# A mixed attention and state-space layer: six of sixteen u*B products on GpSimd, softmax divided after P*V, small norm steps on VectorE, x loaded batch by batch

## Chip, cores and metric
One core of one Trainium2 chip. The time is the device time of one execution in microseconds (us), the median of several runs. The profiled execution is a single one; its span is given beside its time.

## What is computed
Eight independent sequences (batches) of 512 tokens with D = 128 channels, float32. Each goes through one layer of four branches and one feed-forward step:

```
xn    = normalise(x); delta = softplus(xn W_dt + b)          # state-space branch, NS = 64 states
h     = scan over t of  exp(-exp(A_log) delta_t) h + (delta_t xn_t) B_t ;  y_t = sum_n h_tn C_tn
attn  = 16 heads of 8, blocks of 32 queries on 96 keys, softmax(scores + bias) V, then W_o
conv  = silu(4-tap causal convolution);  mem = x W_wm + 0.3 softmax(x dec^T) dec
x1    = x + 0.2 attn + 0.45 (y + x D) W_ssm + 0.15 conv + 0.2 mem
out   = x1 + normalise(x1) W2 + bias                         # W2: quantised kernel plus low rank
```

## The kernel before
**Units and slots.** The recurrence has 128 x 64 = 8192 rows, done as 64 units of 128 rows (two channels with 64 states each). In every batch a unit needs: u = delta*xn of its two channels spread over 64 partitions each (on TensorE, `unit_u`, line 903, into one of four PSUM banks `uP`), the product u*B (`unit_input`, 1182, VectorE), the decay exp(A*delta) (`unit_exp`, 657, ScalarE, from rows that the DMAs `widen`, 393, have written 64 times), the scan itself (`unit_scan`, 1191, VectorE), and the product with C (`pair_product`, 1384, GpSimd, for two units at a time), which TensorE sums (`reduce_group`, 930). Units with s % 4 == 3 do not use TensorE and VectorE for u*B: `widen_u` (382) brings their u by DMA into `uwide`, and `pool_input` (1398) multiplies on GpSimd.

**Order by hand.** Each engine's program goes through slots s = 0..63 of a batch (`body`), and everything else of the layer hangs on a slot: the tables `AT`, `JOB_AT`, `SCORES_AT` and the lags behind a block's scores slot (lines 46 to 78). VectorE's slot s is: waits for scores if a block's bias is due (`scores_there`, 1205), `unit_input(s)`, `unit_scan(s-1)`, then small things: `bias_and_max`, `inverse_sums`, memory softmax, norms. TensorE's slot s begins with `unit_u(s+2)`, which waits for the scan of unit s-2, since the bank is used again; ScalarE's with `unit_exp(s+2)`, which waits for scan s-1. All waits are on counting semaphores, in program order: whatever stands behind a waiting instruction on its engine waits too. Batches 1 to 6 are a loop of three turns with two batches each; batches 0 and 7 stand in front of and behind it.

**Attention.** Block k (of 16) has its scores in slot 6+3k on TensorE (bank `sP`), bias and maximum on VectorE in slot +2, exp on ScalarE in +3 and +4, the inverse of the sums on VectorE in +6 (`inverse_sums`, 1219), the division of all 384 probabilities per query on GpSimd from +5 (`prob_norm`, 1392), transposes on TensorE in +9 and their copy on ScalarE, P*V in +11 and its copy (`ao_copy`, 691). At the end of the batch four matmuls with `wo_p` (`project`, n = 6 to 9, line 998) read the result.

**Norms.** `ln_stats` (1155) and `ln_aggr` on VectorE in slots 0 and 2 treat the next batch's x, `ln_root_step` (1367) does eight 128x4 steps on GpSimd in slots 4 to 7, `ln_apply` (541) follows on ScalarE in slot 11. The second norm: `residual` (1241) in slot 14, `aggr2` 16, `root2` (1407, four steps, GpSimd) 17, `normalise2` (548, ScalarE) 20.

**x.** All eight batches of x are loaded at the start (`x_load`, 353, lines 372 and 373) and stay in SBUF. SyncE issues nearly all DMAs, in one program order: its `front` (475) ends with twelve `window_values` DMAs, and then comes `body`.

Of the kernel before, what the change touches and what calls it, by code (L numbers as in the profile page):

```python
# [5 lines left out]
F32 = mybir.dt.float32  # L6
# [44 lines left out]
LAST_PROJECT = {60: (0, 1), 61: (2, 3), 62: (4, 5), 63: (6, 7)}  # L51
# [5 lines left out]
    "normalise2": 20, "ffn": 25, "output": 29,  # L57

    "ln_stats": 0, "ln_aggr": 2, "ln_root": 4, "ln_apply": 11, "scale_xn": 12, "softplus_exp": 20,
# [8 lines left out]
ROWS_AT = {"store": 15, "rows": 14}  # L68
VALUE_DMA_AT = {4: (0, 1, 2, 3, 4, 5), 5: (6, 7, 8), 6: (9, 10, 11)}
# [7 lines left out]
BIAS_LAG, EXP_LAG, INV_LAG, NORM_LAG, PT_LAG, PT_COPY_LAG, PV_LAG, AO_COPY_LAG = 2, (3, 4), 6, 5, 9, 9, 11, 11  # L77
# [8 lines left out]
def memory_tile_at(s, lag):  # L86
# [7 lines left out]
    ["stats", "aggr", "ve", "nm", "r", "nb", "vr", "vrr", "ve2", "r2", "xa", "xn"])}  # L94
# [4 lines left out]
POOL_Q = 3  # L99
UNIT_PAIRS = UNITS // 2  # L100
# [9 lines left out]
L2 = {n: i + 1 for i, n in enumerate(["x1", "stats", "aggr", "ve", "nm", "r", "nb", "z"])}  # L110
# [5 lines left out]
def hybrid_block_kernel(nc, x, ln_g, ln_b, w_xproj, w_dt, b_dt, A_log, D_ssm, w_ssm_out, wq, wk, wv,  # L116
# [3 lines left out]
    with ctx:  # L120
# [14 lines left out]
        mhalf = sb("mhalf", [128, NT])  # L135
        mone = sb("mone", [128, NT])
        eps_t = sb("eps_t", [128, NT])
# [9 lines left out]
        wo_p = sb("wo_p", [128, REP, D])  # L147
# [32 lines left out]
        x_sb = sb("x_sb", [128, NB, NT, D])  # L180
        st = sb("st", [128, NT, 6])
        mv = sb("mv", [128, NT, 2])
        ve = sb("ve", [128, NT])
        rr = sb("rr", [128, NT])
        vr = sb("vr", [128, NT])
        rr2 = sb("rr2", [128, NT])
        nm = sb("nm", [128, NT])
# [18 lines left out]
        u_rows = nc.dram_tensor("u_rows", [2, 32, L], F32, kind="Internal").ap()  # L206
        uwide = [sb(f"uwide{c}", [128, 2, L]) for c in range(U_SLOTS)]
        q_mask = sb("q_mask", [128, REP])
# [10 lines left out]
        prob = sb("prob", [128, 4, KVH, 3 * W])  # L219
# [3 lines left out]
        ao4 = sb("ao4", [128, REP, L])  # L223
# [16 lines left out]
        nmz = sb("nmz", [128, NT])  # L240
# [4 lines left out]
        x_in = [sem(f"x_in{i}") for i in range(2)]  # L245
# [13 lines left out]
        p_exp, p_inv, p_norm = sem("p_exp"), sem("p_inv"), sem("p_norm")  # L259
        pt_ready, pt_evac, pv_ready, ao_evac = sem("pt_ready"), sem("pt_evac"), sem("pv_ready"), sem("ao_evac")  # L260
# [6 lines left out]
        urows_out, gbx_done = sem("urows_out"), sem("gbx_done")  # L267
        uwide_in = [sem(f"uwide_in{c}") for c in range(U_SLOTS)]
        head_tables = sem("head_tables")
# [13 lines left out]
        def job_count(fam, B, name):  # L283
            return B * COUNT[fam] + INDEX[fam][name] + 1

# [32 lines left out]
        N_FIRST_DMA, N_W_DMA = 13, 18  # L318

        def xin(B):  # L320
            if isinstance(B, int):
                return x_sb[:, B, :, :]
            return x_sb[:, bass.ds(B, 1), :, :].rearrange("p a t d -> p (a t) d")
# [28 lines left out]
        def _(sp):  # L352
            def x_load(b):
                sp.dma_start(x_sb[:, b, :, :], x[b].rearrange("(t p) d -> p t d", p=128)) \
                    .then_inc(x_in[min(b, 1)], 16)

            x_load(0)
# [14 lines left out]
            for b in range(1, NB):  # L372
                x_load(b)


            def store_rows(B, p):

                wait(sp, sp_step, B * N_SP + SP["u"])
                sp.dma_start(dt_rows[p], dtv[:, :]).then_inc(rows_out, 16)
                sp.dma_start(u_rows[p], uv[32 * POOL_Q:32 * POOL_Q + 32, :]).then_inc(urows_out, 16)  # L380

            def widen_u(B, p, m):

                wait(sp, scan_done, B * UNITS + 8 * (m - U_SLOTS) + 8)
                if m == 0:
                    wait(sp, urows_out, (B + 1) * 16)
                flat = u_rows.rearrange("a d t -> (a d t)")
                for j in range(2):
                    row = p * 32 + 4 * m + j
                    src = bass.AP(flat.tensor, flat.offset + row * L, [[0, 64], [2 * L, 2], [1, L]])  # L390
                    sp.dma_start(uwide[m % U_SLOTS][64 * j:64 * j + 64, :, :], src).then_inc(uwide_in[m % U_SLOTS], 16)

# [11 lines left out]
            def body(B, p):  # L404
                for m in range(UNIT_PAIRS):
# [19 lines left out]
            def load_weights():  # L425
# [12 lines left out]
                sp.wait_ge(const_ready, 2)  # L438
                for g in range(KVH):
                    sp.dma_start(wo_p[32 * g:32 * g + HD, :, :],  # L440
                                 wo[g * REP * HD:(g + 1) * REP * HD, :].rearrange("(r h) e -> h r e", r=REP)) \
                        .then_inc(w_in, 16)
                    n += 1
                assert n == N_W_DMA

            def window_values(B, which):
# [4 lines left out]
                else:  # L451
                    wait(sp, s_ready, B * NBLK + 1)
# [22 lines left out]
            def front(B, p):  # L475
# [23 lines left out]
        def _(act):  # L499
# [14 lines left out]
            def setup_step(s):  # L514

                if s == 0:
                    act.wait_ge(w_in, 16 * N_W_DMA)
# [23 lines left out]
            def ln_apply(B):  # L541
                wait(act, ln_step, B * N_LN + LN["r2"])
                for t in range(NT):
                    ins = nc.scalar.activation(xa[:, t, :], xin(B)[:, t, :], ACT.Identity, bias=nb[:, t:t + 1],
# [12 lines left out]
            def scale_xn(B):  # L557
                wait(act, ln_step, B * N_LN + LN["xa"])
                for t in range(NT):
                    ins = nc.scalar.activation(xn[:, t, :], xa[:, t, :], ACT.Copy, scale=rr2[:, t:t + 1])  # L560
# [96 lines left out]
            def unit_exp(B, s):  # L657
# [6 lines left out]
                to = uP[q][:, :] if q == POOL_Q else decay[:, q, :]  # L664
# [9 lines left out]
            def probabilities(B, k, half):  # L674
                if half == 0:
                    wait(act, s_max, B * NBLK + k + 1)
                    wait(act, pt_ready, B * NBLK + k - 3)
                for g in (2 * half, 2 * half + 1):
                    ins = nc.scalar.activation(prob[:, k % 4, g, :], s_sb[:, k % 2, g, :], ACT.Exp,  # L679
# [11 lines left out]
            def ao_copy(B, k):  # L691
                wait(act, pv_ready, B * NBLK + k + 1)
                if k == 0:
                    wait(act, ready["t"], B * N_TAIL - N_TAIL + 1)
                nc.scalar.activation(ao4[:, :, k * W:(k + 1) * W],  # L695
                                     ptP[:, 0:128].rearrange("p (r q) -> p r q", r=REP), ACT.Copy).then_inc(ao_evac, 1)
# [55 lines left out]
            def body(B, p):  # L752
                for s in range(UNITS):
# [6 lines left out]
                    else:  # L760
                        if s == AT["y_copy"]:
# [12 lines left out]
                    k = block_at(s, AO_COPY_LAG)  # L774
                    if k is not None:
                        ao_copy(B, k)
# [27 lines left out]
            def tail(B, p):  # L804
                y_copy(B)
# [8 lines left out]
        def _(pe):  # L814
# [8 lines left out]

            pe.wait_ge(const_ready, 1)
# [6 lines left out]
            def setup_step(s):  # L831

                if s == 0:
                    pe.wait_ge(w_in, 16 * N_W_DMA)
# [68 lines left out]
            def unit_u(B, p, s):  # L903

                i, q = divmod(s, 4)
                if q == POOL_Q:
# [33 lines left out]
            def scores(B, p, k):  # L940
                if k == 0:
                    wait(pe, done["p"], job_count("p", B, "k"))
                wait(pe, s_max, B * NBLK + k)
                mm(sP[:, 0:KVH * 3 * W], q4[:, k, :, :].rearrange("p r q -> p (r q)"), k4[:, :, k * W:k * W + 3 * W],  # L944
                   start=True, stop=True).then_inc(s_ready, 1)

            def prob_transposes(B, k):
                wait(pe, p_norm, B * NBLK + k + 1)
                wait(pe, ao_evac, B * NBLK + k)
# [520 lines left out]
```

## Time and profile before

| | us |
|---|---|
| median of 3 runs (1114.25 to 1122.23) | 1114.3 |
| the profiled execution | 1114.23 |
| its span in the profile | 1112.4 |

So 1.8 us lie around the span. Batches 1 to 6 begin on VectorE at 176, 308, 439, 571, 704 and 834 us, and batch 7 at 963: some 131 to 132 us for each batch, or 2.05 us for a slot. In the profile DVE is VectorE, ACT ScalarE, POOL GpSimd, PE TensorE and SP SyncE; an arrow `<-` in brackets names what ended an idle time.

### The profile page before, as it was taken

The page shows a single profiled execution, that of the slowest core. Times are in us where ns is not written, and L with a number is a line of the kernel's source. Part 1 is how long each engine was busy: PE and PEld are TensorE (multiplying, and loading weights), DVE is VectorE, ACT ScalarE, POOL GpSimd, SP SyncE. Part 2 cuts the span into 40 slices and gives each one's busy share as a digit, 9 for nine tenths or more (in the row PEclk, how much of TensorE's full clock was granted, in tenths as well). Part 3 has the DMA queues.
Part 4 walks back from the last instruction along what each step waited for, and adds up shares of the span by engine and source line. Part 5 has one row for each costly group of instructions (what it writes and reads, how often), then busy time and mean ns, then how long its engine had stood idle before and what let it go on. Part 6 is the DMA issues. An engine that isn't in the chain of part 4 may idle for free. (4 is left out here: it accounts for less than half of the span.)

```text
span 1112.4 us, 19145 instructions
## 1 busy us (share of the span) xinstructions
PE 830.9 (75%) x4151; PEld 339.3 (30%) x4151; DVE 979.3 (88%) x2299; ACT 837.5 (75%) x2255; POOL 955.6 (86%) x675
## 2 busy tenths in 40 slices
PE   5367878688777786877778777867868778677775
PEld 2023333233323332333323333323332333232332
DVE  2688999979997999979999699897999799999991
ACT  4468886788778878687877887679887887858871
POOL 6369988989898988988899898899989898979892
PEclk9556998978997989979898798888899798989897
DMA  5845667647675666666676476665666566766630
GB/s 111 196 126 169 180 159 185 171 138 198 163 183 155 185 167 159 172 157 172 168 203 161 128 191 162 167 173 159 177 176 183 153 187 165 188 161 164 196 95 9
DMA packets 124391, 181.18 MB, mean 163 GB/s; under 512 B 29263, under 2 KB 41056, under 8 KB 124256
## 3 DMA queue, kind: packets, MB, share of 16 engines
q1 hardware_dynamic: 123968, 179.56, 61.4%
q14 instruction: 96, 0.79, 0.3%
q8 instruction: 39, 0.64, 0.3%
q10 hardware_dynamic: 288, 0.20, 0.1%
HBM read 170.79 MB, written 5.05 MB: 158 GB/s over the span
## 5 line engine op out<-in xcount | busy, mean ns | idle before, releaser
L1389 POOL TENSOR_TENSOR prod<-hst,C 128x1024 f32<-128x1024 f32 x256 | 602.0, 2354 | 94.9 <-DVE hst L1201 94.4
L1201 DVE TENSOR_TENSOR_SCAN hst<-decay,bank 128x512 f32<-128x512 f32 x384 | 459.5, 1209 | 3.0 <-DVE cv_a L1236 2.8
L1189 DVE TENSOR_TENSOR bank<-bank,B 128x512 f32<-128x512 f32 x384 | 263.1, 685 | 52.6 <-PE bank L911 34.8
L665 ACT ACTIVATE decay<-wide,A_rep 128x512 f32<-128x512 f32 x384 | 273.4, 715 | 41.5 <-DVE hst L1201 31.2
L911 PE MATMUL bank<-spread,sel_bc 96*128 96x512 bf16 x384 | 164.5, 434 | 101.0 <-DVE hst L1201 90.6
L679 ACT ACTIVATE prob<-s_sb,nmax 128x96 f32<-128x96 f32 x512 | 185.2, 365 | 0.9 <-DVE nmax L1214 0.5
L1405 POOL TENSOR_TENSOR uwide<-uwide,B 128x512 f32<-128x512 f32 x128 | 162.7, 1271 | 22.5 <-DMA uwide<-u_rows 22.5
L935 PE MATMUL bank<-prod,sel_red 128*32 128x512 f32 x1024 | 164.9, 722 | 0.0
L1201 DVE TENSOR_TENSOR_SCAN hst<-bank,uwide 128x512 f32<-128x512 f32 x128 | 155.4, 1214 | 2.7 <-POOL uwide L1405 2.7
L951 PE MATMUL bank<-ident,prob 128*96 128x128 f32 x512 | 85.9, 295 | 77.5 <-ACT ao L695 58.3
L944 PE MATMUL bank<-k,q 128*128 128x384 f32 x256 | 126.7, 580 | 22.3 <-DVE nmax L1214 22.2
L688 ACT ACTIVATE probT<-bank 96x512 f32<-96x512 f32 x128 | 74.9, 585 | 72.0 <-PE bank L951 71.6
L911 PEld LDWEIGHTS bank<-spread,sel_bc 96*128 96x128 bf16 x384 | 40.2, 106 | 228.0 <-DVE hst L1201 176.5
L665 ACT ACTIVATE bank<-wide,A_rep 128x512 f32<-128x512 f32 x128 | 87.2, 681 | 26.8 <-DVE hst L1201 26.6
L1394 POOL TENSOR_TENSOR prob<-prob,pinv 128x384 f32<-128x384 f32 x128 | 105.8, 826 | 0.0
L951 PEld LDWEIGHTS bank<-ident,prob 128*96 128x96 f32 x512 | 61.3, 137 | 135.4 <-issue 102.6
L1214 DVE CUSTOM_DVE_ANT_0 s_sb<-bank,bias 128x96 f32<-128x96 f32 x512 | 98.3, 250 | 0.0
L679 ACT ACTIVATION_READ_ACCUMULATOR prob<-s_sb,nmax 128x1 f32 x512 | 98.1, 192 | 0.0
L944 PEld LDWEIGHTS bank<-k,q 128*128 128x128 f32 x256 | 48.9, 216 | 87.0 <-DVE nmax L1214 48.6
L959 PE MATMUL bank<-probT,vw 96*8 96x128 f32 x1024 | 57.0, 298 | 14.7 <-ACT probT L688 9.8
L695 ACT ACTIVATE ao<-bank 128x128 f32<-128x128 f32 x128 | 34.1, 266 | 30.8 <-PE bank L959 30.5
L959 PEld LDWEIGHTS bank<-probT,vw 96*8 96x8 f32 x1024 | 19.9, 94 | 89.5 <-issue 57.1
(189 smaller groups left out, 1027.4 us busy)
## 6 DMA issues: line engine op xcount, KB each, us to landing
wide<-dt_rows SPq DMA_DIRECT2D x512, 256.0 KB, 4.7
uwide<-u_rows SPq DMA_DIRECT2D x128, 256.0 KB, 4.1
spread<-parts SPq DMA_DIRECT2D x66, 32.0 KB, 4.1
x_sb<-in_L_attn_x_dram SPq DMA_DIRECT2D x8, 256.0 KB, 4.5
dt_rows<-sp_t SPq DMA_DIRECT2D x8, 256.0 KB, 2.6
out_dram<-outb SPq DMA_DIRECT2D x8, 256.0 KB, 3.9
vw<-v_tok SPq DMA_DIRECT2D x80, 16.0 KB, 3.3
u_rows<-uv SPq DMA_DIRECT2D x8, 64.0 KB, 2.4
```

The costliest lines, as they stand in the source:

```text
L665: nc.scalar.activation(to, wide[m % SLOTS][:, s % 2, :], ACT.Exp, scale=A_rep[:, g:g + 1]).then_inc(exp_done, 1)
L679: ins = nc.scalar.activation(prob[:, k % 4, g, :], s_sb[:, k % 2, g, :], ACT.Exp, bias=nmax[:, k % 2, g:g + 1], scale=-1.0, accum_out=psum ...
L911: mm(uP[q][:, :], sel_bc[:, i, :, :].rearrange("k j n -> k (j n)"), spread[p][:, q, :], start=True, stop=True).then_inc(u_ready, 1)
L935: ins = mm(yP[32 * q:32 * q + 32, :], sel_red[:, i, :], prod[:, (i % 2) * 4 + q, :], start=(i == 0), stop=(i == GROUPS - 1), skip_group_ch ...
L944: mm(sP[:, 0:KVH * 3 * W], q4[:, k, :, :].rearrange("p r q -> p (r q)"), k4[:, :, k * W:k * W + 3 * W], start=True, stop=True).then_inc(s_ ...
L951: ins = nc.tensor.transpose(ptP[0:3 * W, g * 128:(g + 1) * 128], prob[:, k % 4, g, :], ident[:, :])
L1189: v.tensor_tensor(uP[s % 4][:, :], uP[s % 4][:, :], B2[p][:, :], ALU.mult).then_inc(dbx_done, 1)
L1201: v.tensor_tensor_scan(hst[:, s % 8, :], kept, into[:, :], 0.0, ALU.mult, ALU.add).then_inc(scan_done, 1)
L1214: ins = v.tensor_tensor_reduce(s_sb[:, k % 2, g, :], sP[:, g * 3 * W:(g + 1) * 3 * W], bias3[:, row, g, :], 1.0, BIG, ALU.add, ALU.min, nm ...
L1389: g.tensor_tensor(prod[:, 2 * (m % 4):2 * (m % 4) + 2, :], hst[:, 2 * (m % 4):2 * (m % 4) + 2, :], C2[p][:, :].unsqueeze(1).to_broadcast([ ...
L1394: g.tensor_tensor(prob[:, k % 4, :, :], prob[:, k % 4, :, :], pinv[:, k % 4, :].unsqueeze(2).to_broadcast([128, KVH, 3 * W]), ALU.mult) \
L1405: g.tensor_tensor(u, u, B2[p][:, :], ALU.mult).then_inc(gbx_done, 1)
```

## The change
- GpSimd takes u*B of the units s % 8 == 5 as well (24 of 64, before 16). Their u comes through a second DRAM table and `widen_odd` into `uodd`. In each batch that is eight products more on GpSimd, and eight products fewer on VectorE and eight matmuls fewer on TensorE. In an odd slot GpSimd does `pair_product`, then the product of unit s+4 (in slots s % 8 == 1), then that of s+6 (in slots s % 4 == 1).
- GpSimd's division of the probabilities goes. P*V runs on raw exponentials at lag 8 (transposes at lag 6), `raw_copy` takes it to SBUF, TensorE turns it (`turn`, lag 10) into the unused fourth quarter of the bank `sP`, and VectorE divides 32 values per query (`output_norm`, lag 11). At the end of the batch `heads` transposes back, `heads_copy` copies, and sixteen matmuls of 128 columns replace four of 512.
- Because the turned block lies in the bank of the scores, VectorE's `scores_there` also waits for `turned`, from the fourth block on.
- `inverse_sums` moves from lag 6 to 8.
- The norms' steps, all but the power, go to VectorE: `ln_vars` (slots 4 to 7), `ln_shift` (10), `vars2` (16), `shift2` (20); GpSimd keeps one power for each norm (slots 7 and 17). `ln_stats` moves to slot 1, `ln_apply` to 12, `normalise2` to 21.
- x is kept for one batch: SyncE loads x of the next batch at the start of `body`, and x again into `x1` for the residual in its step 21.
- The output weights go to a larger tile `wo4`, cleared on VectorE and loaded by 16 DMAs at the end of SyncE's `front`.

```diff
+def on_pool(s):
+    return s % 4 == 3 or s % 8 == 5
...
-BIAS_LAG, EXP_LAG, INV_LAG, NORM_LAG, PT_LAG, PT_COPY_LAG, PV_LAG, AO_COPY_LAG = 2, (3, 4), 6, 5, 9, 9, 11, 11
+BIAS_LAG, EXP_LAG, INV_LAG, PT_LAG, PT_COPY_LAG, PV_LAG, RAW_COPY_LAG, TURN_LAG, NORM_LAG = 2, (3, 4), 8, 6, 6, 8, 8, 10, 11
+TURN_AHEAD = 3
...
-            for b in range(1, NB):
-                x_load(b)
...
             def body(B, p):
+                if not last(B):
+                    x_load(B + 1, x_sb, x_in)
                 for m in range(UNIT_PAIRS):
...
+                    if m % 8 == 7:
+                        if m // 8 + 2 < 4:
+                            widen_odd(B, p, m // 8 + 2)
+                        elif not last(B):
+                            widen_odd(B + 1, 1 - p, m // 8 - 2)
...
+                    if m == ROWS_AT["residual"]:
+                        x_load(B, x1, xres_in)
...
                 for m in range(U_SLOTS):
                     widen_u(B, p, m)
+                    widen_odd(B, p, m)
                 for at in VALUE_DMA_AT.values():
                     window_values(B, at)
+                load_output_weights()
...
+            def turn(B, k):
+                wait(pe, raw_evac, B * NBLK + k + 1)
+                wait(pe, ao_norm, B * NBLK + k)
+                nc.tensor.transpose(sP[:, KVH * 3 * W:], ao_raw[:, k % 2, :], ident[:, :]).then_inc(turned, 1)
...
             def ln_stats(B):
-                dve.wait_ge(x_in[0], 16)
-                if not first(B):
-                    dve.wait_ge(x_in[1], 16 * (NB - 1))
+                wait(dve, x_in, B * 16 + 16)
...
                 wait(dve, s_ready, B * NBLK + k + 1)
                 wait(dve, p_exp, B * NBLK + k - 1)
+                if k >= TURN_AHEAD:
+                    wait(dve, turned, B * NBLK + k - TURN_AHEAD + 1)
...
+            def output_norm(B, k):
+                wait(dve, turned, B * NBLK + k + 1)
+                wait(dve, p_inv, B * NBLK + k + 1)
+                wait(dve, heads_ready, B)
+                v.tensor_tensor(ao_q[:, k, :].rearrange("p (g h) -> p g h", h=HD),
+                                sP[:, KVH * 3 * W:].rearrange("p (g c) -> p g c", c=W)[:, :, 0:HD],
+                                pinv[:, k % 4, :].unsqueeze(2).to_broadcast([128, KVH, HD]), ALU.mult).then_inc(ao_norm, 1)
...
+            def shift2(B):
+                wait(dve, l2_step, B * N_L2 + L2["r"])
+                v.scalar_tensor_tensor(nbz[:, :], mv2[:, :, 0], -1.0, rz[:, :], ALU.mult, ALU.mult).then_inc(l2_step, 1)
```

## Rows read from the trace of the kernel before
**Rows 1.** The page, part 1: busy time, share of the span, instructions
```profile
PE 830.9 (75%) x4151; PEld 339.3 (30%) x4151; DVE 979.3 (88%) x2299; ACT 837.5 (75%) x2255; POOL 955.6 (86%) x675
```
**Rows 2.** Waits of VectorE over the whole span: total us, times, longest
```profile
DVE bank L1189 <- PE bank L911: 34.8, 24, 8.1
DVE pinv L1222 <- ACT prob L679: 25.3, 8, 3.8
DVE bank L1189 <- PE bank L944: 14.3, 14, 2.4
```
**Rows 3.** Groups of instructions by line and shape: busy us, mean ns | idle before
```profile
L1189 DVE TENSOR_TENSOR bank<-bank,B 128x512 f32<-128x512 f32 x384 | 263.1, 685 | 52.6 <-PE bank L911 34.8 <-PE bank L944 14.3 <-issue 1.8
L1405 POOL TENSOR_TENSOR uwide<-uwide,B 128x512 f32<-128x512 f32 x128 | 162.7, 1271 | 22.5 <-DMA uwide<-u_rows 22.5
L1394 POOL TENSOR_TENSOR prob<-prob,pinv 128x384 f32<-128x384 f32 x128 | 105.8, 826 | 0.0
L1375 POOL TENSOR_TENSOR rr<-ve,mhalf 128x4 f32<-128x4 f32 x8 | 8.1, 1014 | 0.1
L1222 DVE RECIPROCAL pinv<-psum_r 128x4 f32<-128x4 f32 x128 | 20.0, 156 | 25.3 <-ACT prob L679 25.3
```
**Rows 4.** Timeline of VectorE at the start of batch 4: start, us, instruction
```profile
569.81 1.20 DVE L1201 TENSOR_TENSOR_SCAN hst<-bank,uwide 128x512 f32<-128x512 f32 x1
571.51 0.86 DVE L1160 BATCH_NORM_STATS2 st<-x_sb 128x6 f32 x4
...
579.58 0.70 DVE L1189 TENSOR_TENSOR bank<-bank,B 128x512 f32<-128x512 f32 x1 [0.70 <-PE bank L911]
...
585.47 0.70 DVE L1189 TENSOR_TENSOR bank<-bank,B 128x512 f32<-128x512 f32 x1 [0.69 <-PE bank L911]
```
**Rows 5.** Timeline of SyncE at the same place, and where the loop turns (437 us)
```profile
571.04 1.22 SPq L391 DMA_DIRECT2D uwide<-u_rows  x2
...
437.59 1.23 SPq L391 DMA_DIRECT2D uwide<-u_rows  x2
443.47 6.02 SPq L402 DMA_DIRECT2D wide<-dt_rows  x8
```
**Rows 6.** Line 354, the eight loads of x: from issue to landing
```profile
DMA to landing us min/median/max: 2.9/4.5/6.4
```
**Rows 7.** Timeline of SyncE in the front
```profile
22.04 1.36 SPq L440 DMA_DIRECT2D wo_p<-in_L_attn_wo_dram x4
...
37.38 2.55 SPq L391 DMA_DIRECT2D uwide<-u_rows  x4
40.05 8.43 SPq L456 DMA_DIRECT2D vw<-v_tok  x12
```
**Rows 8.** Timeline of VectorE in batch 0
```profile
40.39 0.17 DVE L1115 MEMSET bias<- 128x128 f32 x1
...
46.96 1.22 DVE L1201 TENSOR_TENSOR_SCAN hst<-bank,uwide 128x512 f32<-128x512 f32 x1 [2.73 <-POOL uwide L1405]
...
51.52 1.45 DVE L1121 TENSOR_SCALAR wo_p<-wo_p 128x512 f32<-128x512 f32 x1
...
63.05 0.29 DVE L1133 TENSOR_REDUCE wmax<-wf_abs 128x1 f32<-128x128 f32 x1 [2.60 <-ACT wf_abs L532]
```
**Rows 9.** Timeline of batch 3: GpSimd's product of slot 17, VectorE's first of slot 21
```profile
475.95 2.36 POOL L1389 TENSOR_TENSOR prod<-hst,C 128x1024 f32<-128x1024 f32 x1 [2.12 <-DVE hst L1201]
...
479.28 0.70 DVE L1189 TENSOR_TENSOR bank<-bank,B 128x512 f32<-128x512 f32 x1
```
**Rows 10.** Timeline of TensorE in slots 39 and 40 of batch 3, then VectorE in slot 41
```profile
524.27 0.60 PE L951 MATMUL bank<-ident,prob 128*96 128x128 f32 x4
524.71 1.88 PE L967 MATMUL bank<-xaT,convdiag 128*128 128x512 f32 x4
526.42 0.38 PE L911 MATMUL bank<-spread,sel_bc 96*128 96x512 bf16 x1
...
525.66 0.68 DVE L1189 TENSOR_TENSOR bank<-bank,B 128x512 f32<-128x512 f32 x1
```

More of the change, by code:

```diff
@@ L99, with products @@
 POOL_Q = 3
+def on_pool(s):
+    return s % 4 == 3 or s % 8 == 5
+def products(s, pool):
+    return sum(on_pool(t) == pool for t in range(s + 1))
+N_POOL = sum(on_pool(s) for s in range(64))
+N_VEC = 64 - N_POOL
 UNIT_PAIRS = UNITS // 2
@@ L146, in hybrid_block_kernel @@
         wk_s = sb("wk_s", [D, KVH * HD])
-        wo_p = sb("wo_p", [128, REP, D])
+        wo4 = sb("wo4", [128, 4, REP, D])
         w_ssm = sb("w_ssm", [D, D])
@@ L436, in load_weights, with load_output_weights @@
                     n += 1
[L438 to L443, printed above, removed]
-                assert n == N_W_DMA
+                assert n == N_W_DMA
+            def load_output_weights():
+                sp.wait_ge(wo_clean, 1)
+                for c in range(4):
+                    for g in range(KVH):
+                        sp.dma_start(wo4[32 * c + g * HD:32 * c + g * HD + HD, c, :, :],
+                                     wo[g * REP * HD:(g + 1) * REP * HD, :].rearrange("(r h) e -> h r e", r=REP)) \
+                            .then_inc(w_in, 16)
             def window_values(B, which):
@@ L689, in probT_copy, with raw_copy, heads_copy @@
                     .then_inc(pt_evac, 1)
-            def ao_copy(B, k):
+            def raw_copy(B, k):
                 wait(act, pv_ready, B * NBLK + k + 1)
[L693 to L696, printed above, removed]
+                wait(act, turned, B * NBLK + k - 1)
+                nc.scalar.activation(ao_raw[:, k % 2, :], ptP[:, 0:128], ACT.Copy).then_inc(raw_evac, 1)
+            def heads_copy(B):
+                wait(act, heads_ready, B + 2)
+                nc.scalar.activation(aoT[:, :, :, :].rearrange("p c r q -> p (c r q)"), ptP[:, :], ACT.Copy,
+                                     scale=RW_ATTN).then_inc(heads_evac, 1)
             def mem_exp(B, t):
@@ L960, in values, with heads @@
                 ins.then_inc(pv_ready, 1)
+            def turn(B, k):
+                wait(pe, raw_evac, B * NBLK + k + 1)
+                wait(pe, ao_norm, B * NBLK + k)
+                nc.tensor.transpose(sP[:, KVH * 3 * W:], ao_raw[:, k % 2, :], ident[:, :]).then_inc(turned, 1)
+            def heads(B):
+                wait(pe, ao_norm, (B + 1) * NBLK)
+                transposes([ao_q[:, 4 * a:4 * a + 4, :].rearrange("p k c -> p (k c)") for a in range(4)], 128, 128, ptP) \
+                    .then_inc(heads_ready, 1)
             def conv_tap(B, p, tap):
@@ L998, in project @@
                 elif n < 10:
-                    wait(pe, ao_evac, (B + 1) * NBLK)
-                    ins = mm(jobP[:, :], wo_p[:, n - 6, :], ao4[:, n - 6, :], start=False, stop=False)
+                    wait(pe, heads_evac, B + 1)
+                    c = n - 6
+                    for r in range(REP):
+                        ins = mm(jobP[:, :].rearrange("p (a c q) -> p a c q", a=4, c=4)[:, :, c, :], wo4[:, c, r, :],
+                                 aoT[:, :, r, :], start=False, stop=False, skip_group_check=True)
                 else:
@@ L1056, in body @@
                         values(B, p, k)
+                    k = block_at(s, TURN_LAG)
+                    if k is not None:
+                        turn(B, k)
+                    if s == UNITS - 1:
+                        heads(B)
                     for tap in range(TAPS):
@@ L1073, in tail @@
             def tail(B, p):
-                for n in range(8, N_PROJ - 1):
+                for n in range(6, N_PROJ - 1):
                     project(B, p, n)
@@ L1176, in front @@
                 ln_aggr(B)
+                for n in range(4):
+                    ln_vars(B, n)
+                ln_shift(B)
                 first_tables()
@@ L1289, in body @@
                         inverse_sums(B, k)
+                    k = block_at(s, NORM_LAG)
+                    if k is not None:
+                        output_norm(B, k)
                     t = memory_tile_at(s, M_MAX_LAG)
@@ L1315, in tail @@
                 aggr2(B)
+                vars2(B)
+                shift2(B)
                 output(B)
@@ L1416, in body @@
                         pair_product(B, p, s // 2)
-                    if s % 4 == 1:
-                        if s // 4 + 1 < GROUPS:
-                            pool_input(B, p, s // 4 + 1)
-                        elif not last(B):
-                            pool_input(B + 1, 1 - p, 0)
-                    k = block_at(s, NORM_LAG)
-                    if k is not None:
-                        prob_norm(B, k)
+                    for ahead in (4, 5, 6):
+                        t = s + ahead
+                        if s % 2 == 1 and (t == s + 6 and t % 4 == 3 or t == s + 4 and t % 8 == 5):
+                            if t < UNITS:
+                                pool_input(B, p, t)
+                            elif not last(B):
+                                pool_input(B + 1, 1 - p, t - UNITS)
                     if not first(B):
```

216 lines of the change are left out of this document (123 added, 93 removed).

## Prediction
> **What bounds the kernel now.** Read the page's part 1 first: VectorE is busy 88% of the span, GpSimd 86%, ScalarE and TensorE 75% [rows 1]. Two engines near 90% leave open which one paces the other, so next come VectorE's waits over the span. The reader is to see that none of the large ones is for GpSimd: 34.8 us for TensorE's spread of u (8.1 of it in the front), 25.3 for the exponentials (one wait in each batch, at the inverse of the sums), 14.3 for the scores [rows 2]. GpSimd on its side waits for scans, once 2.12 us [rows 9]. So VectorE paces the body, disturbed by a late TensorE and ScalarE, and GpSimd follows. A microsecond taken from GpSimd is worth nothing by itself; one taken from VectorE is worth one, as long as TensorE and ScalarE can follow; and each new wait in VectorE's program costs in full.
>
> **Part 1, VectorE's own work.** Eight products fewer in each batch. One lasts 0.685 us [rows 3], but the next instruction starts 0.58 after it, so 8 x 0.59 = 4.7 us go. Sixteen `output_norm` of 128x32 come. No row has one; below is the reciprocal of 128x4, 0.156 long and about 0.07 from start to start, above the product of 512 elements at 0.59. The work is nearest to the small one, 32 elements: I take 0.09, so 1.4; the range for sixteen is 1.1 to 3. The norms bring seven small steps at 0.07 to 0.15, 0.7 with one self-wait. Net -2.5 us per batch, -20 over eight.
>
> **Part 2, GpSimd.** It loses sixteen divisions (0.826), gains eight products (1.271) and loses one of three powers (1.01) and nine smaller steps: -13.2 + 10.2 - 1.0 = -4 us per batch, and a little more for the small steps [rows 3]. As VectorE does not wait for it, I cost this at nothing. The cover: the product of unit s+4 ends 2.3 + 1.2 = 3.5 us after scan s, and scan s+4 starts four slots of 2.05 us less its own 1.2 later, 7 us. The Trainium skill (GPSIMD Engine Reference, "Performance versus the Vector engine") speaks against handing such work over: elementwise work should stay on VectorE, GpSimd takes about twice as long. The trace agrees, 1.271 against 0.685 [rows 3]; but the rule prices the engine, and here the dearer microseconds fall on the engine that nobody waits for.
>
> **Part 3, x arrives late.** Until now x was in SBUF. Now its load stands at the start of SyncE's `body`, behind `widen_u` and `widen_odd` of step 31, and the former waits for the last scan of the batch. In batch 4 that scan ends at 571.0 and SyncE issues at 571.04, two DMAs in 1.22 us [rows 4, 5]. Four DMAs, then x: issued at 573.5. x landed in 2.9 to 6.4 us, median 4.5 [rows 6]; with four 256 KB transfers ahead of it I take 4.0: 577.5. VectorE reaches `ln_stats` in slot 1, after one product and one scan more than before: 571.51 + 0.58 + 1.13 = 573.2. It stands for 4.2 us. At the turn of the loop (two of six) SyncE resumed its next DMA only 4.65 us after the end of the last [rows 5]; if that is the turn itself, x comes that much later, some 7 us of waiting. Batch 1 about 3. Sum over batches 1 to 6: 3 + 3 x 4.2 + 2 x 7 = 29.6. Some comes back: while VectorE stands, TensorE works off its projections, and its three waits behind them (the first 0.70, the last 0.69, one of 0.45 between) go [rows 4]: -10. Net +20; both ends: +6 (landing in 2.9 and no turn penalty) and +32. The Trainium skill's page on DMA (DMA: Bandwidth & Descriptors, "Rules for kernel authors") says to issue early and wait late; the change issues and waits within 3 us. No rule of it changes the sum.
>
> **Part 4, batch 0.** This one is larger than any other and the surest. x of batch 1 is now issued after all of SyncE's front. Before, that was four `uwide` DMAs from 37.38 and twelve `vw` in 8.43 us. Now it is eight of the former (4 x 0.61 more), then sixteen of `wo4` at 0.34, 5.4 us [rows 7]: 37.4 + 4.9 + 8.4 + 5.4 = 56.1, landing at about 60. VectorE is ready for it when its bias tables are done, 40.5 less the 0.8 of statistics, 39.7 [rows 8]. It stands for 20 us. Given back: its later waits for `uwide` (2.73) and for `wf_abs` (2.60), whose causes catch up meanwhile, and the scaling of `wo_p` (1.45) [rows 8]; also about 1 us of a shorter norm in the front. +12.6, I take +13, with ends +8 and +18.
>
> **Part 5, the middle of a batch.** The wait of 3.2 us per batch for exponentials goes with lag 8 [rows 2]. But ScalarE is then some microseconds behind with the decays as well, so most of it moves to the scans of units 24 and 25. And `shift2` adds a wait: GpSimd starts the product of slot 17 at 475.95, then two products and the power, 2.3 + 1.2 + 1.2 + 1.0, so 481.7; VectorE ends slot 20 at 479.28 + 0.2 [rows 3, 9]: 2.2 us, eased by ScalarE's catching up. I take -3 over all batches; ends -22 and +8.
>
> **Part 6, the turned block.** `scores_there` stands ahead of `unit_input` and now wants TensorE's work of the slot just before, not of two slots before. Slot 41 shows it: TensorE ends the transposes at 524.9, does two convolution taps until 526.6, then u; a turn behind that ends at about 527.1, and VectorE starts slot 41 at 525.66 [rows 10]: 1.45 us. By the same reading the eight blocks from slot 32 on would wait 0.7, 0, 0, 1.45, 0.9, 0, 0.75 and 0.2, together 4 us; where a reduction (1.06 us) or taps precede the turn it is late. VectorE's halts let TensorE catch up, and eight spreads fewer help, so I take 1.5 per batch, +12; ends 0 and +32. TensorE gets 16 turns, 4 transposes and the finer projection, some 5 us less 3.5 for eight spreads, which matter only through this wait.
>
> **Tail.** Transposes (0.60 for four [rows 10]) and one copy of about 0.6 stand between the last block and the projection: +2.
>
> **Sum.** -20 + 0 + 20 + 13 - 3 + 12 + 2 = +24. The profiled execution took 1114.2 and the median is 1114.3, so either base gives **1138 us**.
>
> **The rivals.** (a) *VectorE's gain counts and the waits are absorbed* (faster). After each wait for x the other engines are ahead, so the body runs at VectorE's pace: -20 and -22 (the exponentials' wait), x at 0, front +13, tail +2: -27, 1087 us. For it: VectorE waits in a batch for nothing but late TensorE and ScalarE [rows 2]. Against: what can be absorbed behind x is 1.8 us [rows 4]. It decides if less than 1 us of the 4.2 is left at slot 8. (b) *The turn is never late* and the exponentials' wait goes whole: -20 + 20 + 13 - 22 + 10 (`shift2`) + 0 + 2 = +3, 1117 us, no change. For it: TensorE idles a quarter of the span [rows 1]. (c) *The turn is late whenever the rows say so* and x at its upper end: -20 + 32 + 15 + 32 - 3 + 2 = +58, 1172 us. (d) *The change does not relieve VectorE*: the division reads a bank that TensorE is about to write, and at 0.6 each sixteen would cost 9.6 us and undo part 1: 1138 + 65 = 1203; against it, the reciprocal costs 0.07. I give it 1 in 100.
>
> **How the numbers follow.** Forecast 1138 (from 1125.5 to 1155): 0.54. (b): 0.20. (a): 0.13. (c) and beyond: 0.13. Within 1% (1103 to 1125.5), about what a measurement of this kernel can tell from no change, lies (b); faster is (a), slower the forecast and (c). The range leaves out the far halves of (a) and (c): 1104 to 1165.
>
> **What would show it.** In the changed profile: one wait of VectorE's statistics for the DMA of x, some 20 us long, at about 40 us, and six of 3 to 8 us; a new wait for the turned block, 1 to 2 us at a time, in slots with a reduction or taps; a wait for GpSimd's power once in a batch, near 2 us; the wait at `pinv` gone; `output_norm` near 0.15 us long; GpSimd's share of the span lower. Wrong if x has landed when VectorE asks (parts 3 and 4 fall), or if VectorE's waits for TensorE shrink by more than the turn adds (part 6).

## The result, and the profile after
Four runs of the changed kernel took 1226.0 to 1237.6 us, median 1230.3, against 1114.8 for the kernel before beside them: ratio 1.103, 95% interval [1.096, 1.110]. The prediction was 1138, range 1104 to 1165, so the sign was right and the size was not: +116 us where +24 was said. The profiled execution took 1230.0, its span is 1228.1.

The page's part 1 of the changed kernel, which answers to [rows 1]:
```profile
PE 858.0 (70%) x4439; PEld 375.4 (31%) x4439; DVE 1007.4 (82%) x2419; ACT 848.5 (69%) x2263; POOL 917.8 (75%) x528
```
VectorE was to lose 20 us of work and gained 28, and its idle time grew by 88. The whole loss, 28 of work and 88 of idle time, can be read on VectorE. Its waits, which answer to [rows 2] (total us, times, longest):
```profile
DVE st L1230 <- DMA x_sb<-in_L_attn_x_dram: 60.1, 7, 19.0
DVE bank L1281 <- PE bank L1020: 57.6, 34, 4.9
DVE bank L1281 <- PE bank L961: 32.8, 15, 8.3
DVE nbz L1370 <- POOL rz L1522: 12.7, 8, 2.1
```
The first is x, the second the turned block (L1020 is `turn`), the third the spread of u as before, the fourth `shift2`. Of the two old waits, that for the exponentials (25.3) is gone and that for the scores (14.3) is down to 0.7. Three waits of TensorE, over the whole span:
```profile
PE bank L961 <- DVE hst L1293: 147.1, 108, 22.8
PE bank L995 <- DVE ao_q L1322: 73.6, 58, 2.5
PE bank L1012 <- DMA vw<-v_tok: 36.2, 7, 5.9
```
The spread of u (L961) waits for VectorE's scans, as before (there 90.6); new are the other two: the scores (L995) wait for `output_norm`, which itself waits for `turn`, and P*V waits once in a batch for its values (4.7 us in all before). The groups of VectorE's work that changed, answering to [rows 3]:
```profile
L1281 DVE TENSOR_TENSOR bank<-bank,B 128x512 f32<-128x512 f32 x320 | 219.6, 687 | 94.4 <-PE bank L1020 57.6 <-PE bank L961 32.8 <-DVE outb L1374 1.5
L1322 DVE TENSOR_TENSOR ao_q<-bank,pinv 128x32 f32<-128x32 f32 x128 | 20.8, 163 | 0.0
L1370 DVE SCALAR_TENSOR_TENSOR nbz<-mv,rz 128x4 f32<-128x4 f32 x8 | 16.2, 2031 | 12.7 <-POOL rz L1522 12.7
L1365 DVE TENSOR_SCALAR vz<-mv 128x4 f32<-128x4 f32 x8 | 15.2, 1905 | 0.3
L1252 DVE TENSOR_SCALAR vv<-vi 128x4 f32<-128x4 f32 x8 | 7.9, 994 | 0.0
L1246 DVE TENSOR_SCALAR vv<-mv 128x4 f32<-128x4 f32 x8 | 5.4, 680 | 0.0
L1250 DVE TENSOR_TENSOR vi<-mv,vi 128x4 f32<-128x4 f32 x8 | 4.6, 571 | 0.0
L1258 DVE SCALAR_TENSOR_TENSOR nb<-mv,rr 128x4 f32<-128x4 f32 x8 | 1.3, 162 | 1.8 <-POOL rr L1492 1.8
L1248 DVE RECIPROCAL vi<-vv 128x4 f32<-128x4 f32 x8 | 1.2, 150 | 0.0
```
Products fell by 43.5 us of busy time and `output_norm` is as cheap as said, but steps on four elements take up to 2 us. The same form, SCALAR_TENSOR_TENSOR on 128x4, takes 162 ns in one line and 2031 in another, so it isn't the form of the instruction. What it stands for shows when VectorE's line is laid beside GpSimd's. Timeline of VectorE (start, us), slot 20 of batch 4:
```profile
689.05 2.29 DVE L1370 SCALAR_TENSOR_TENSOR nbz<-mv,rz 128x4 f32<-128x4 f32 x1 [2.07 <-POOL rz L1522]
```
and of GpSimd:
```profile
688.00 1.01 POOL L1522 TENSOR_TENSOR rz<-vz,mhalf 128x4 f32<-128x4 f32 x1
688.98 2.34 POOL L1505 TENSOR_TENSOR prod<-hst,C 128x1024 f32<-128x1024 f32 x1
```
The small step is released by the power, but GpSimd has already gone on to a product; that ends at 691.32 and the step at 691.34. Of the Trainium skill, the page "SBUF — State Buffer" (section "SBUF: two separate sides") has the rule: VectorE and GpSimd share one pair of SBUF ports, and when a VectorE instruction with two SBUF inputs or in a two-port mode meets a GpSimd instruction that reads SBUF, whichever started first keeps the pair to its end. The trace agrees to 0.02 us here. It is a rule that spoke against this change and that the prediction did not weigh.

### The profile page after: what moved, and what is told of

Its sections match the earlier page's. It is cut to its first block and busy times, and to the rows that moved or that the text cites. A ratio compares the mean times of both kernels' runs of the same rounds, so it can differ in the third digit from the quotient of the medians.

```text
span 1228.1 us, 20161 instructions
## 1 busy us (share of the span) xinstructions
PE 858.0 (70%) x4439; PEld 375.4 (31%) x4439; DVE 1007.4 (82%) x2419; ACT 848.5 (69%) x2263; POOL 917.8 (75%) x528
## 5 line engine op out<-in xcount | busy, mean ns | idle before, releaser
L1293 DVE TENSOR_TENSOR_SCAN hst<-decay,bank 128x512 f32<-128x512 f32 x320 | 384.5, 1209 | 11.5 <-issue 3.3
L1281 DVE TENSOR_TENSOR bank<-bank,B 128x512 f32<-128x512 f32 x320 | 219.6, 687 | 94.4 <-PE bank L1020 57.6
L707 ACT ACTIVATE decay<-wide,A_rep 128x512 f32<-128x512 f32 x320 | 229.9, 719 | 44.0 <-DVE hst L1293 34.2
L961 PE MATMUL bank<-spread,sel_bc 96*128 96x512 bf16 x320 | 142.8, 447 | 162.5 <-DVE hst L1293 147.1
L707 ACT ACTIVATE bank<-wide,A_rep 128x512 f32<-128x512 f32 x192 | 131.6, 685 | 102.4 <-DVE hst L1293 101.1
L995 PE MATMUL bank<-k,q 128*128 128x384 f32 x256 | 126.9, 581 | 78.5 <-DVE ao_q L1322 73.6
L961 PEld LDWEIGHTS bank<-spread,sel_bc 96*128 96x128 bf16 x320 | 34.8, 109 | 265.7 <-DVE hst L1293 232.1
L1004 PEld LDWEIGHTS bank<-ident,prob 128*96 128x96 f32 x512 | 65.2, 141 | 88.9 <-issue 61.7
L995 PEld LDWEIGHTS bank<-k,q 128*128 128x128 f32 x256 | 46.1, 212 | 142.3 <-DVE nmax L1308 109.2
L1517 POOL TENSOR_TENSOR uodd<-uodd,B 128x512 f32<-128x512 f32 x64 | 81.2, 1269 | 0.0
L1293 DVE TENSOR_TENSOR_SCAN hst<-bank,uodd 128x512 f32<-128x512 f32 x64 | 77.6, 1213 | 0.0
L737 ACT ACTIVATE ao_raw<-bank 128x128 f32<-128x128 f32 x128 | 34.3, 268 | 42.8 <-PE bank L1012 42.3
```

The lines of the kernel that those rows point to most:

```text
L707: nc.scalar.activation(to, wide[m % SLOTS][:, s % 2, :], ACT.Exp, scale=A_rep[:, g:g + 1]).then_inc(exp_done, 1)
L961: mm(uP[q][:, :], sel_bc[:, i, :, :].rearrange("k j n -> k (j n)"), spread[p][:, q, :], start=True, stop=True).then_inc(u_ready, 1)
L1004: ins = nc.tensor.transpose(ptP[0:3 * W, g * 128:(g + 1) * 128], prob[:, k % 2, g, :], ident[:, :])
L1281: v.tensor_tensor(uP[s % 4][:, :], uP[s % 4][:, :], B2[p][:, :], ALU.mult).then_inc(dbx_done, 1)
L1293: v.tensor_tensor_scan(hst[:, s % 8, :], kept, into[:, :], 0.0, ALU.mult, ALU.add).then_inc(scan_done, 1)
L1517: g.tensor_tensor(pool_slot(s), pool_slot(s), B2[p][:, :], ALU.mult).then_inc(gbx_done, 1)
```

## The experiments
The first four undo one thing each in the changed kernel (1230.3). Each ratio is to the kernel before, run beside it on the same chip; its median beside these groups of runs was 1112.3 to 1116.7, so that a few us between medians of different groups are noise. e1 to e4 have two executions each.

**e1, x early.** x is issued two batches ahead, in SyncE's step 25; batch 1's in the front. For that SyncE's loop has two turns in place of three, with batches 5 and 6 written out behind it (in e6 to e11 and e13 to e16 as well).
```diff
-                if not last(B):
-                    x_load(B + 1, x_sb, x_in)
...
+                    if m == 25 and not (isinstance(B, int) and B + 2 > NB - 1):
+                        x_load(B + 2, x_sb, x_in)
```


> The changed kernel, but x of the batch after next is loaded half a batch ahead (SyncE's step 25, and in the front right behind the weights) into the same single tile. Theory (each of the seven waits of VectorE for x, 60.1 us in all, is paid by the whole kernel, and some 10 us come back while the others catch up): the waits for x fall to nothing, the time falls by 45 to 60 us, to about 1175. Rival (the body is held by TensorE's turned block anyway, and a wait for x is only one way to spend that time): the waits for the turned block grow by what the waits for x lose, the time falls by less than 20 us.

Measured 1186.5 (1.067 [1.057, 1.078]): 44 us, a little under the theory's 45. The waits for x are gone; VectorE's waits for the turned block stay (61.6 and 8.2), and its setup now waits 6.4 us for the late `wo4`.

**e2, the norms' steps back on GpSimd.** The helpers of the kernel before, from slot 5.

> The changed kernel with the norms' small steps back on GpSimd, eight and four of them, everything else as changed. Theory (on VectorE some of these 128x4 steps stand until GpSimd's running instruction ends: 0.7 to 2.3 us instead of 0.15, 6.5 us per batch, and the shift of the second norm waits 1.6 more for the power): VectorE's busy time falls by some 45 us, the time by 45 to 60 us, to about 1180. Rival (VectorE had that time to spare, since it waits for the turned block and for x): less than 20 us.

Measured 1220.9 (1.098 [1.090, 1.106]): the rival. The medians differ by 9 us, the ratios by 5, and the intervals overlap. VectorE's busy time fell from 1007.4 to 960.0, as the rule of the port says, but other waits took its place; VectorE's waits of this run:
```profile
DVE bank L1265 <- PE bank L1025: 67.2, 36, 5.1
...
DVE hst L1277 <- PE bank L1025: 24.1, 8, 4.2
...
DVE hst L1277 <- ACT decay L712: 16.2, 7, 2.7
DVE hst L1277 <- POOL uodd L1490: 11.2, 6, 2.2
```
Here 91 us stand for the turned block (L1025), against 61 in the changed kernel: while the turn is late, VectorE's freed time is only waited away.

**e3, the wait for the turn behind product and scan.**
```diff
-                if k >= TURN_AHEAD:
-                    wait(dve, turned, B * NBLK + k - TURN_AHEAD + 1)
...
+                if TURN_AHEAD - 2 <= k < NBLK - 2:
+                    wait(dve, turned, B * NBLK + k)
                 v.reciprocal(pinv[:, k % 4, :], psum_r[:, k % 4, :]).then_inc(p_inv, 1)
```
(`inverse_sums` now stands ahead of `bias_and_max`.)

> The changed kernel, but VectorE waits for the turned block only right ahead of the bias, behind the slot's product and scan, so 1.1 to 1.7 us later. Theory (TensorE is late by 1.7 us on average over 34 waits): most of the 57.6 us of waits goes, the time falls by 30 to 50 us, to about 1190. Rival (TensorE itself is behind by whole slots, so that what is not waited for here is waited for at the next spread of u or scores): the waits move to the spread of u and the time falls by less than 15 us.

Measured 1191.9 (1.072 [1.069, 1.075]): the theory, 38 us for a wait moved by two instructions. The waits for the turn fell from 60.9 to 22.9:
```profile
DVE pinv L1315 <- PE bank L1020: 22.9, 12, 3.9
```

**e4, the values' transfers early.** `VALUE_DMA_AT = {0: (0, 1, 2, 3), 1: (4, 5, 6, 7), 2: (8, 9, 10, 11)}`.

> The changed kernel, but the twelve DMAs of the value windows are issued in SyncE's steps 0 to 2, ahead of the wait of step 3 for the eighth scan. Theory (P*V of block 0 comes three slots sooner than before, its data do not, TensorE stands 5 us per batch, 36.2 us in all, and VectorE behind it at the turned block): TensorE's wait goes, the time falls by 15 to 30 us, to about 1208. Rival (TensorE has time to spare there): within 5 us of the changed kernel.

Measured 1218.6 (1.096 [1.092, 1.100]): 12 us between the medians, 7 by the ratios, whose intervals overlap; less than the theory's 15, and not clear of noise. TensorE's wait for `vw` is gone.

**e5, the norms' small steps alone, on the kernel before.** With them come the slots of the change: `ln_apply` 12 and `normalise2` 21, one later than before.

> The kernel before with one part of the change alone: the norms' small steps on VectorE, one power each on GpSimd. Nothing else is late here that could hide their cost. Theory (VectorE's 128x4 steps stand until GpSimd's running instruction ends): the seven steps cost 5 to 6.5 us per batch here too, so VectorE's busy time rises by 35 to 50 us and the time by 25 to 50: 1137 to 1162. Rival (what the norms cost is taken back from VectorE's waits for TensorE and ScalarE, as the 9 us of the norms' removal from the changed kernel suggest): VectorE's busy time rises alike, its waits of 130 us fall by as much, and the time stays within 1% of the kernel before: 1103 to 1123.

Measured 1138.4 (1.022 [1.019, 1.025]): +23 us. That is inside the theory's 1137 to 1162, 2 us short of its 25 to 50, and clearly outside the rival's. VectorE's busy time rose by 44 and the wait for the power brought 15 more; its waits for the spread of u, the exponentials and the scores fell by 36. How much of the 23 comes from ScalarE's norms standing a slot later is not shown; e14 will show that one such slot can matter.

**e6 and e7, all four delays mended together** (x, turn, values, and `wo4` loaded during batch 0 with a semaphore of its own), in e7 with the norms on GpSimd as well.

> The changed kernel with the four delays mended together: x two batches ahead, the wait for the turned block behind product and scan, the vw transfers in SyncE's first steps, and wo4 loaded during batch 0; the norms stay on VectorE, GpSimd keeps six of sixteen. Theory of separate causes (each alone gave -44, -38 and -12; wo4 6 more): 1230 - 100 = 1130, between 1120 and 1145. Rival (they are one queue of VectorE's waits, and each mends partly what another would): 1150 to 1175.

> The same with the norms' steps back on GpSimd. Theory (the norms gave only 9 us alone since x, the turn and late transfers took their place; with these gone they give what they cost VectorE, 40 us): 40 below the run beside it, 1080 to 1100. Rival (GpSimd, with six products and all norm steps, is now late with its products): within 10 us of the run beside it, with VectorE's waits for GpSimd's products and TensorE's waits for prod above 25 us.

e6 took 1134.4 (1.019 [1.016, 1.022]), e7 1117.8 (1.000 [0.998, 1.003]). So the delays nearly add up: e1, e3 and e4 gave 44 + 38 + 12, the wait for `wo4` in e1 was 6, and together 96 went. The norms' steps are worth 17 us where x, turn and transfers are not late, with all slots alike, not the 40 said: in e7 VectorE's busy time is 958.1 (e6: 1006.0), and new waits stand there:
```profile
DVE hst L1289 <- ACT decay L722: 23.4, 8, 4.1
DVE bank L1277 <- PE bank L976: 20.3, 14, 8.5
DVE hst L1289 <- PE bank L1010: 20.0, 8, 3.9
DVE hst L1289 <- POOL uodd L1502: 12.8, 7, 2.2
```
The decay comes late once in a batch, the scores once, GpSimd's new product once. TensorE's waits for `prod` are 30.7, over the rival's 25, but the time is neither side's.

**e9, four of sixteen on GpSimd,** otherwise e7 (x issued three of SyncE's steps later). Of the change the division after P*V, with its `wo4` and the second load of x, is left, and the later slots of the norms with it. (e8, the same with x in step 24, has no measured time.)

> As the kernel with all delays mended and the norms on GpSimd, and GpSimd forms u*B of four of sixteen, as before (and x is issued three of SyncE's steps later); of the change the division after P*V is left. Theory (VectorE paces, and eight products in a batch are worth 4.7 us to it): 25 to 40 us slower than the run with six of sixteen, which took 1117.8: 1143 to 1158. Rival (with six of sixteen GpSimd is the later engine, and its products make VectorE wait for what they save): within 10 us of 1117.8, or faster.

Measured 1129.3 (1.011 [1.008, 1.015]): six of sixteen is worth 11.5 us here, between theory and rival, with 34 us less of VectorE's busy time (991.9 to 958.1). e9 itself is 14.6 above the kernel before. The division after P*V is the largest part of the change left in it, but no run separates it from the second load of x, the later `inverse_sums` and the norms' ScalarE steps one slot later.

**e10 and e11, the small steps where GpSimd is idle.** From e6: the first norm's four steps together in slot 5, `vars2` in slot 17 (`"vars2": 17`) in place of 16. In e11 the second norm's steps are on GpSimd besides.

> As the run with the four delays mended and the norms on VectorE (1134.4), with the same steps at other slots: the first norm's four together in slot 5 and the second's variance in slot 17, where GpSimd has only a pair's product under way, some 0.3 us from its end, in place of slots 4 to 7 and 16, where a product starts with the scan that VectorE has just ended. Theory (a small step stands until GpSimd's running instruction ends): the variance of the second norm falls from 2.15 us to 0.3 to 0.6, the three steps of the first norm from 0.74 + 0.57 + 0.99 to 0.9 in all; VectorE's busy time falls by 20 to 25 us and the time by 10 to 25: 1110 to 1124. Rival (the steps are slow by themselves on VectorE, or the wait is for something else of the slot): durations as before within 20%, and the time within 5 us of 1134.

> As the run beside it, with all of the second norm's steps on GpSimd, so that its last step, which follows GpSimd's power and starts just as GpSimd goes on with a product, is no longer VectorE's (2.0 us long, and 1.9 us of waiting for the power, in each batch). Theory: VectorE is freed of 30 us, GpSimd gains few small steps, and the time falls by 15 to 30 more: 1085 to 1105, below the kernel before. Rival (VectorE's waits for TensorE and ScalarE take it back, as when the norms left the changed kernel): within 8 us of the run beside it.

e10 took 1138.6 (1.019 [1.013, 1.026]), e11 1130.7 (1.011 [1.004, 1.018]). The mechanism held and the forecast of time did not: e10 is within 5 us of e6 (1134.4) and e11 within 8 of e10, as the rivals said. The tile `vz` in e10 (min/median/max ns), an instruction whose median was 2146 in e6:
```profile
L1377 DVE TENSOR_SCALAR vz<-mv x8: 158/160/170, 219.0 to 1124.1; 128x4 f32<-128x4 f32 x8
```
Timelines of e10 in slot 5, VectorE, then GpSimd:
```profile
593.36 0.89 DVE L1258 TENSOR_SCALAR vv<-mv 128x4 f32<-128x4 f32 x1
594.29 0.18 DVE L1260 RECIPROCAL vi<-vv 128x4 f32<-128x4 f32 x1
594.50 2.05 DVE L1262 TENSOR_TENSOR vi<-mv,vi 128x4 f32<-128x4 f32 x1
...
606.13 2.31 DVE L1270 SCALAR_TENSOR_TENSOR nb<-mv,rr 128x4 f32<-128x4 f32 x1 [0.67 <-POOL rr L1506]
```
```profile
592.95 1.28 POOL L1531 TENSOR_TENSOR uwide<-uwide,B 128x512 f32<-128x512 f32 x1
594.18 2.36 POOL L1519 TENSOR_TENSOR prod<-hst,C 128x1024 f32<-128x1024 f32 x1
```
The first step ends with the product under way (594.25 and 594.23), the reciprocal passes beside a running product in 0.18, and the next step, with two SBUF inputs, stands until that product ends (596.55 and 596.54). The first step and the reciprocal have one SBUF input each; what parts them would by the rule be a two-port mode of TENSOR_SCALAR, which no view here shows. My slot 5 was read as idle and wasn't; `nb`, 0.16 long before, now follows the power and meets a product. What `vz` gained, these lost: VectorE's busy time is 1008.8 (e6: 1006.0). e11's waits for decays and scores (22.4 and 20.0) are those of e7.

**e12 and e13, one delay put back into e9:** x as the change loads it, and the turn's wait as the change places it.

> As the run with four of sixteen and all delays mended (1129.3), with x loaded where the change loads it: at the start of SyncE's body, for the next batch. Prediction's terms: 20 us of waiting in batch 0 and 3 to 8 in each of the others, net +33, so 1162 (between 1145 and 1180). Theory from the changed kernel (x alone is worth what it was worth there, 44 to 50): 1173 to 1180. Rival (its cost came from meeting the late turn and the slow norm steps; with SyncE's queue shorter and ScalarE's and TensorE's waits elsewhere most is given back): under 1150.

> As the same run (1129.3), with VectorE's wait for the turned block where the change has it, ahead of product and scan. The prediction's term: +12, 1141 (rows' own reading +32, 1161). Theory from the changed kernel: +38, 1167. Rival (the turn is late there only since x and the norm steps put ScalarE and TensorE out of step): within 8 us of 1129.

e12 took 1142.5 (1.025 [1.022, 1.028]), the rival; e13 took 1173.0 (1.050 [1.046, 1.053]), above the theory's 1167. Alone, x costs 13 of its 33.7 us of waiting (10.6 in batch 0, 2.9 to 5.4 in the others, where the changed kernel has 19.0 and 6.1 to 7.7); alone, the turn costs 44. VectorE's wait for the turn in e13:
```profile
DVE bank L1270 <- PE bank L1028: 80.1, 49, 4.0
```
TensorE's wait for `output_norm` in e13, then in e9:
```profile
PE bank L1003 <- DVE ao_q L1311: 61.5, 48, 2.5
```
```profile
PE bank L1003 <- DVE ao_q L1311: 29.4, 39, 1.6
```
One of e13's waits for the turn ends at 581.24, after 2.06 us; TensorE's timeline ahead of it:
```profile
575.80 1.81 PE L993 MATMUL bank<-prod,sel_red 128*32 128x512 f32 x8
577.54 1.65 PE L1003 MATMUL bank<-k,q 128*128 128x384 f32 x2
578.99 0.81 PE L1012 MATMUL bank<-ident,prob 128*96 128x128 f32 x4
579.63 1.06 PE L1054 MATMUL bank<-mdiag,mprob 128*128 128x128 f32 x8
580.52 0.38 PE L969 MATMUL bank<-spread,sel_bc 96*128 96x512 bf16 x1
580.74 0.27 PE L1028 MATMUL bank<-ident,ao_raw 128*128 128x128 f32 x1
```
A reduction, scores, transposes and memory products, 5 us in one piece, stand ahead of 0.27 us of turn.

**e14, a try at ScalarE's burst:** e7 with `"normalise2": 22`.

> As the run with six of sixteen and all mended (1117.8), with ScalarE's second normalisation (1.6 us) in slot 22 in place of 21, behind the softplus logarithm and its two table loads. Theory (VectorE's 2.9 us wait for a decay in each batch stands behind that burst): the wait falls by 1 to 1.6 us in each batch and the time by 5 to 15: 1103 to 1113, below the kernel before. Rival (the burst is as long as before, and what is gained is lost one slot later): within 4 us of 1117.8.

Measured 1131.0 (1.014 [1.011, 1.017]), worse than both sides' numbers: the decay's wait fell from 23.4 to 14.7 us, but TensorE's transposes of z, in slot 23, now wait 27.9 us for the normalised block, and scores come later (27.1 + 18.3).

**e15 and e16, turn and division one slot earlier** (lags 9 and 10), on e7 and on e13. Once in a batch TensorE's `turn` also waits for the last block's maximum (`s_max`).
```diff
-... RAW_COPY_LAG, TURN_LAG, NORM_LAG = 2, (3, 4), 8, 6, 6, 8, 8, 10, 11
+... RAW_COPY_LAG, TURN_LAG, NORM_LAG = 2, (3, 4), 8, 6, 6, 8, 8, 9, 10
```


> As the run with six of sixteen and all mended (1117.8), with the turn in lag 9 and the division of its block in lag 10, each a slot earlier, so that TensorE's scores need not wait for the division of the slot before (43 us of TensorE's waits) and VectorE's for scores and turned block shrink (20 + 10 + 6 us). Theory: half to all of these 36 us go, less what ScalarE's late copy now costs TensorE: 1090 to 1110, below the kernel before. Rival (scores are late because of TensorE's own work in those slots, or the earlier turn waits for ScalarE's copy of the same slot): within 6 us of 1117.8, or slower.

> As the run with four of sixteen and the early wait (1173.0), with the turn and the division a slot earlier; the wait stays ahead of product and scan. Theory (the turn was a slot too near its wait): VectorE's wait for the turn falls from 80 us to under 20, and the time to 1125 to 1140. Rival (the place of the wait as such, or the earlier turn itself waits for ScalarE's copy of the raw block): above 1155, with the wait for the turn over 50 us.

e15 took 1120.5 (1.003 [1.001, 1.006]): the rival, no gain where the wait is already late; 41.5 us of VectorE's waiting now stand at the division itself. e16 took 1136.2 (1.018 [1.014, 1.023]), 37 us less than e13. With the turn a slot earlier the early wait costs 7 us more than the late one (e9), not 44. TensorE's wait for `output_norm` is gone from its list. The theory's time held, its wait didn't: in the profiled execution, the slowest of six at 1145.1, 43.9 us for the turn remain, but at the end of a slot, behind product and scan:
```profile
DVE ao_q L1313 <- PE bank L1030: 43.9, 33, 3.6
```

## Why the prediction was wrong, point by point
- **What bounds the kernel**: VectorE paces, right; "GpSimd costs nothing" (part 2) was not. e10 and e5 show GpSimd's running instruction setting the length of VectorE's (in e5 a step that starts at 584.93 ends at 585.71, GpSimd's product at 585.68), which no row of waits names, since it counts as busy time.
- **Part 1, -20**, was mis-sized on both sides. The norms' steps were priced at 0.7 per batch, 6 us; they took 51.8 of busy time and 17 (e6 against e7) to 23 us (e5, with the later slots) of the span. The eight products were priced at 4.7 per batch, 38 us; they gave 11.5 (e9 against e7): of the 34 us that VectorE's work lost, 24 came back as idle time, 12.8 of it for `uodd` and some 6 more each for the turn and for decays. `output_norm` was right: 163 ns long.
- **Part 2, 0**: its cover was nearly enough; in e7 `uodd` is waited for 12.8 us, but only with all norm steps on GpSimd.
- **Parts 3 and 4, +33.** The 20 us of batch 0 were right (19.0; the terms that the prediction takes off leave 12.2, not 12.6). The loop's turn was right too: at both turns x is issued late and the waits were 7.7 and 6.9, where 7 was said. What failed is the landing in the other four batches, taken at 4.0: there VectorE starts on x 5.7 to 7.5 us after its issue, and the four waits are 26.5 in all, not 15.6. SyncE's timeline at a turn of the loop, then in batch 4:
```profile
486.98 1.91 SPq L419 DMA_DIRECT2D uodd<-u_rows  x2
493.76 0.41 SPq L373 DMA_DIRECT2D x_sb<-in_L_attn_x_dram  x1
...
635.30 1.25 SPq L419 DMA_DIRECT2D uodd<-u_rows  x2
636.75 0.44 SPq L373 DMA_DIRECT2D x_sb<-in_L_attn_x_dram  x1
```
and VectorE's statistics at the same two places:
```profile
496.54 0.87 DVE L1230 BATCH_NORM_STATS2 st<-x_sb 128x6 f32<-128x128 f32 x4 [7.71 <-DMA x_sb<-in_L_attn_x_dram]
...
644.07 0.87 DVE L1230 BATCH_NORM_STATS2 st<-x_sb 128x6 f32<-128x128 f32 x4 [6.18 <-DMA x_sb<-in_L_attn_x_dram]
```
At the turn SyncE pauses for 4.9 us ahead of x, which is there 2.8 after its issue; in batch 4, issued right behind four transfers, it takes 7.3. That these four transfers are the reason is likely, not shown apart: in e12, with two ahead, it takes 4.8 to 5.3. Undone in the changed kernel x was worth 44 us, alone 13. The net depends on the waits beside it, and 33 lies between.
- **Part 5, -3**: the exponentials' wait went, and that for the power is 2.07 at 689.05 (2.2 said), 12.7 over all batches. Not seen: the step behind it is then 2.3 us long in place of 0.16.
- **Part 6, +12**: the step that failed most, and the largest miss. It measured 38 (e3) and 44 (e13). The rows gave 4.0 per batch, and I took 1.5, as VectorE's halts would let TensorE catch up. They did not: the halt stands ahead of a scan, and TensorE's next spread waits for that scan, the scores for `output_norm`, and that for the turn (TensorE's wait for `ao_q`: 29.4 us in e9, 61.5 in e13). So each engine passes its delay back to the other, and even 32 was too low. This ring is read from the program and the waits; e16 supports it, since one slot opens it and 37 of the 44 us go.
- **Left out**: the twelve `vw` DMAs. P*V moved from slot 17 to 14 in block 0, while its DMAs moved only from SyncE's step 4 to 3, still behind `widen_u`'s wait for the eighth scan: some 7 to 12 us (e4).
- **The rivals**: all four lie below 1205 and none had two mechanisms feeding each other; (c) had the right two causes at too low a price. (b)'s "the turn is never late" and (a)'s absorption fell with e3 and e1. Taken off in this one order, the +116 are 96 for the delays of x, turn, `vw` and `wo4` (changed kernel against e6), 17 for the norms' steps (e6 against e7), -11.5 for the products (e7 against e9) and +15 for the rest (e9). No version beat the kernel before, the best equals it.
- **The prediction's sum with the measured sizes**: products -11.5 for -38, norms 17 for 6, turn 38 for 12, x 44 for 33, `vw` 12 for 0 add 86 to its 24. That gives 110 of the 116, as a check only, since the sizes come from different company. The tail was not measured apart.
- **Still open**: how the 96 divide, since each delay's worth changed with its company (x: 44 or 13), and what of e9's +15 is the division.

## What to carry to other kernels
When a step goes to another engine, look at what the neighbour on its port runs at that moment, and give VectorE's small steps that read and write SBUF a place where GpSimd waits; a trace shows this as one form with two durations. Place a new wait behind the work that others wait for (e3), or give a transpose that returns to its sender one slot more (e16); with the first done, the second gave nothing (e15). Judge a mended delay only with its neighbours mended too: the norms gave 5 to 9 us of the 52 of their busy time while the turn was late, and 17 when it was not.

## What the hardware showed that was not expected
- TENSOR_SCALAR, TENSOR_TENSOR and SCALAR_TENSOR_TENSOR on 128x4 from SBUF took 0.13 to 0.17 us beside an idle GpSimd (`vz` in e10, the ratio `vi` in e5, `nb` in the changed kernel) and up to 2.3 beside a product; RECIPROCAL, with one input, and `output_norm`, whose first input is in PSUM, stayed at 0.15 to 0.18 and 0.16. A 0.16 us step thus costs up to a whole GpSimd instruction.
- The granted TensorE clock, a mean between the two levels of 1.2 and 2.4 GHz, was 0.871 before, 0.841 after, 0.876 in e9 and 0.839 in e13. A reduction's matmul took 700 ns in e9 and 738 in e13. How long TensorE waits does not order the kernels: e10, with 139.3 us of waiting for scans and 38.0 for `output_norm`, got 0.882. The clock is the smaller part of the 44 us of e13: its execution at a clock of 0.869 took 1168.2, and two of e9 at 0.871 took 1130.0 and 1131.6, so that 37 us or more are left at nearly the same clock.
- GpSimd's power on 128x8 took 1.65 us in the changed kernel, against 1.01 on 128x4 [rows 3].
